# Projection stage of a graph transformer: where ScalarE copies the next turn's normalised features, and where it loads the table of the square root

## What is computed

```
xn  = _layernorm(x, ln1_g[l], ln1_b[l])
deg = (deg - deg.mean()) / (jnp.std(deg, ddof=1) + 1e-06)
pos = xn @ Wpos[l] + bpos[l] + deg[:, None] * Wdeg[l][0] + bdeg[l]
xp  = xn + pos
q   = (xp @ Wq[l] + bq[l]).reshape(n, H, HD)          # k and v alike, by Wk and Wv
att = clip(einsum('ehd,ehd->eh', q[dst], k[src]) / scale, -50, 50)
ex  = exp(att - m[dst])                                # summed and weighted by target node
...
x   = x + (aggr @ Wo[l] + bo[l])
h   = gelu(_layernorm(x, ln2_g[l], ln2_b[l]) @ W1[l] + b1[l])
x   = x + (h @ W2[l] + b2[l])
```

## Time and profile before

| what | before |
|---|---|
| median of 3 runs | 6860.24 us (6857.8 to 6868.34) |
| profiled execution, its own time | 6853.69 us |
| its span in the trace | 6851.9 us |
| busy share PE / DVE / ACT / POOL | 78% / 64% / 43% / 45% |
| projection stage of layer 0 in the span | about 2400 to 2575 us |
| projection stage of layer 1 in the span | about 3885 to 4043 us |

### The profile page before, as it was taken

The page is one execution under the profiler, slowest core; times in us unless marked ns, Lnnn a source line. Parts: engine busy times, 40 slices in busy tenths (PEclk is TensorE's granted clock), DMA queues, the critical chain, the costliest instruction groups (busy, mean ns, idle before and its releaser), DMA issues. The chain is left out here.

```text
span 6851.9 us, 123614 instructions
## 1 busy us (share of the span) xinstructions
PE 5331.7 (78%) x28313; PEld 3586.6 (52%) x28314; DVE 4415.0 (64%) x13076; ACT 2974.1 (43%) x5625; POOL 3066.0 (45%) x3096
## 2 busy tenths in 40 slices
PE   7987995887887656666675767666666999999998
PEld 3443443666666545555554556555555444444433
DVE  8999997888877578888886478888875111000000
ACT  2542551777777325666665335555554000000000
POOL 3763772777777007777773027777760000000000
PEclk9999996999999768999998878899988999999999
DMA  1000002555556216777775036666670677777799
GB/s 24 0 3 1 0 3 62 181 181 180 181 180 167 59 35 211 225 224 224 223 223 116 10 103 205 204 205 206 205 181 30 236 288 288 268 288 286 305 421 388
DMA packets 464533, 1168.30 MB, mean 171 GB/s; under 512 B 112062, under 2 KB 175102, under 8 KB 432156
## 3 DMA queue, kind: packets, MB, share of 16 engines
q1 hardware_dynamic: 337228, 892.75, 35.2%
q0 software_dynamic: 124928, 273.12, 16.2%
q10 hardware_dynamic: 2256, 0.89, 0.1%
HBM read 759.86 MB, written 405.30 MB: 170 GB/s over the span
## 5 line engine op out<-in xcount | busy, mean ns | idle before, releaser
L720 POOL DMA_INDIRECT ACC<-tab_kv,STAGE x1664 | 1632.5, 981 | 1248.5 <-DMA STAGE<-IDX 717.3
L926 PE MATMUL PS<-ITEM 128*128 128x512 f16 x1456 | 590.8, 406 | 585.1 <-ACT PS L1242 583.1
L1242 ACT ACTIVATE PS<-PS,X 128x512 f32<-128x512 f32 x1456 | 964.1, 662 | 167.2 <-PE PS L926 107.3
L720 POOL DMA_INDIRECT SCR<-tab_h,STAGE x832 | 804.9, 967 | 319.1 <-issue 197.8
L1083 PE MATMUL PS<-ACC,Q 128*128 128x512 f32 (+3 forms) x2548 | 843.3, 576 | 49.1 <-DMA ACC<-adj 39.5
L1746 DVE TENSOR_TENSOR ACC<-ACC,PS 128x137 f32 (+1 forms) x2288 | 745.9, 326 | 202.8 <-PE PS L918 68.8
L896 PE MATMUL PS<-Q,SCR 128*128 x4992 | 734.2, 293 | 92.3 <-issue 91.5
L787 PE MATMUL PS<-Q 128*128 128x416 f16 x4160 | 758.1, 341 | 60.5 <-DVE Q L1540 60.5
L896 PEld LDWEIGHTS PS<-Q,SCR 128*128 128x128 f32 x4992 | 682.6, 205 | 208.1 <-issue 184.8
L681 POOL DMA_INDIRECT placed<-ACC,X x576 | 606.6, 1053 | 408.0 <-DVE X L1517 219.5
L914 PE MATMUL PS<-SCR 128*128 128x137 f32 x3328 | 569.2, 321 | 194.7 <-DVE ACC L1746 194.7
(11 more groups left out here) (297 smaller groups left out, 7571.7 us busy)
## 6 DMA issues: line engine op xcount, KB each, us to landing
ACC<-adj SPq DMA_DIRECT2D x252, 1792.0 KB, 6.8
adj<-X SPq DMA_DIRECT2D x936, 256.0 KB
adj<-ITEM SPq DMA_DIRECT2D x520, 256.0 KB
ACC<-tab_kv,STAGE POOLq DMA_INDIRECT x1664
SCR<-tab_h,STAGE POOLq DMA_INDIRECT x832
tab_kv<-SCR SPq DMA_DIRECT2D x14, 896.0 KB, 4.1
ACC<-adj SPq DMA_DIRECT2D x21, 448.0 KB, 3.8
placed<-ACC,X POOLq DMA_INDIRECT x576, 2.3
```

The source lines that it names most:

```text
L720: nc.gpsimd.indirect_dma_start(G[:, q, j, 0:w], None, table, bass.IndirectOffsetOnAxis(STAGE[:, u, q * S4 + j:q * S4 + j + 1], 0))\
L926: nc.tensor.matmul(CLASS_SUM[k % 2], OHS1[:, k % ring, :], OHD[:, k % ring, :], start=False, stop=True, skip_group_check=True).then_inc(ad ...
L1242: nc.scalar.activation(CLASS_SUM[(k + 1) % 2], CLASS_SUM[k % 2], ACT.Copy, scale=KEEP[:, bass.ds(i, 1)])\
```

## The change

One column `ROOT` is allocated. On ScalarE, in both layers, the copy to `T1` of the next turn moves from the head of a loop turn to a place ahead of the exponent (so it is now the copy of turn g + 2 and not of g + 1), the first of these copies moves ahead of the loop, and the one behind the loop goes. At the loop's head a square root of one constant column is taken into `ROOT`, which nothing reads.

```
@@ -156,6 +156,7 @@
+        ROOT = sb("ROOT", [P, 1])[:, :]
@@ -1331,12 +1332,13 @@
                 copied(T1, R[0], s, "xt", "xtc", 0, **norm1)
                 copied(T7, R[0], s, "pt", "ptc", 0)
                 deviation(s, 1)
+                copied(T1, R[0], s, "xt", "xtc", 1, **norm1)
                 with act.Fori(0, NG - 2) as g:
-                    copied(T1, R[0], s, "xt", "xtc", g + 1, **norm1)
+                    nc.scalar.activation(ROOT, EPS[:, 0:1], ACT.Sqrt)
                     copied(T7, R[0], s, "pt", "ptc", g + 1)
                     deviation(s, g + 2)
+                    copied(T1, R[0], s, "xt", "xtc", g + 2, **norm1)
                     self_exp(g)
-                copied(T1, R[0], s, "xt", "xtc", NG - 1, **norm1)
                 copied(T7, R[0], s, "pt", "ptc", NG - 1)
                 self_exp(NG - 2)
                 self_exp(NG - 1)
```

## The result

| | before | changed |
|---|---|---|
| median | 6860.28 us (6857.8 to 6868.34, 6 runs) | 6835.82 us (6830.15 to 6838.42, 6 runs) |
| ratio | | 0.9963, 95% interval 0.9953 to 0.9973 |
| profiled execution, span | 6853.69, 6851.9 | 6835.00, 6833.2 |
| both projection stages, from the traces | 322.94 us | 297.80 us |

The account below looks back on a forecast made before the run. Engines waiting for each other in a ring bound the projection stages, with two VectorE waits in it. Copy 22.2 plus root 7.2 gave 29.4 us less: 6824.3 from the profiled execution, 6830.8 for the median, range 6822 to 6846.

Parts of the forecast that it names:

- What bounds: In the projection stages VectorE waits for the position product (16.1, 16.3 us) and, at the reciprocal, the root (5.5, 5.4 us).
- the ring: In the two projection stages engines wait for each other; none is full, and VectorE waits least.
- The copy, moved: Copy to T1 ahead of the exponent: ten VectorE waits for the position product fall from 24.2 to 2.0, gaining 22.2 us.
- I take 0.2 a turn, 2.0 in all: VectorE's wait left for the position product after the copy moves, over ten turns; bounds 0 and 13 us.
- these two bracket the runs that I looked at: On TensorE, the clock rises between 3.3 and 4.45 us into an unbroken run.
- The bound of 1.3 us a turn: VectorE's wait for the position product if TensorE's clock stays low through that product.
- The root's table: Load hidden in ScalarE's idle time behind the exponent; wait at the reciprocal falls from 1.14 to 0.37 us, gaining 7.2 us.
- The exponent in hand: On ScalarE, moved copy and exponent's table load end 3.0 us before the scores are ready, so they cost nothing.
- The 6.8 us for break-even: Lateness of the transposes ahead of the exponent beyond which the kernel is slower: 3.0 slack plus 3.8 gained a turn.
- The low-clock rival: TensorE's clock stays low through the position product: only 15.9 us less, 6844 us; chance 0.11.
- No gain, and slower: Two rivals: work hidden anyway or wait renamed, 6860 us, chance 0.06; exponent late behind the moved copy, 6872, chance 0.03.

Follow-up runs that it names:

- copy alone: Changed kernel without the early root, only the copy to T1 moved: both stages 301.87 us, median 8851.06 us, ratio 0.9974 to the kernel before.
- root alone: Kernel before with only the early root, put behind the copy to T1: both stages 312.42 us, median 8860.45 us, ratio 0.9987.
- runs with more loads: Changed kernel with two or four more table loads a loop turn, ahead of the exponent: both stages 295.76 and 323.04 us, ratios to before 0.9963 and 0.9994.

## Why the prediction was right or wrong

The forecast was 29.4 us less and 24.5 came, inside the range. By the waits, 3.3 us of the difference lie in the copy's part and 1.1 in a term left out.

- **What bounds.** Right. VectorE's two waits were the ones in the ring; each alone gives its part (21.1 and 10.6 us of stage time), and together 25.1 to 25.4. The parts sum to 31.7, 6.3 us more than both together, because the position waits hang on the clock: 1.4 us in the copy alone and 5.2 in the changed kernel, 20.2 with the root alone and 22.7 to 24.2 before.
- **The copy, moved.** The mechanism was right, and its size was off. The step that failed is "I take 0.2 a turn, 2.0 in all": it was 0.53 a turn, 5.3 us in all. It rested on "these two bracket the runs that I looked at", 3.3 and 4.45 us into the run, and they did not even bracket those of before: one rise was 3.1 us into its run (3950.84 to 3953.9), and in turn 2 of layer 0 (wait 1.90 us) the clock stood high when the run began at 2460.9, fell at 2462.3 and rose again at 2465.7. And both distances were taken from runs that started 5.2 us behind kv, with the product with Wq ahead of them, while the runs of the changed kernel start at kv. In the changed kernel the clock rose 2.9 to 6.2 us into the ten runs of the loop turns. The range held because it went up to the low-clock case; how much was lost inside it is where the rises happened to fall. The bound of 1.3 us a turn held: it was reached in the last loop turn of layer 1 (1.30). The gain was 18.9 and not 22.2 us.
- **A term left out.** The last products also run at the clock that they find. L1903 waits 2.4 us when the run takes 6.55 us and 3.5 us when it takes 7.69, 1.1 us lost in layer 1. The prediction named this wait and gave it no term.
- **The root's table.** Right to 0.1 us: 7.2 us, 0.37 us a time. The load and the new root (0.20 us) lay in ScalarE's idle time.
- **The exponent in hand.** Right: 2.99 us for 3.0. The runs with more loads show that it is 3 us and that beyond it every us is paid. The 6.8 us for break-even added the gain of the one turn shown (3.8); by the prediction's own sum the mean was 29.4 / 10 = 2.9, which gives 5.9, and 6.0 was measured.
- **The low-clock rival** came true in part, as a mixture over turns (it was named so): one turn in ten at its full price, six at 0.4 to 0.9 us, three at nothing.
- **No gain, and slower.** Neither came. The exponent could be made late, by 6.0 us of extra work ahead of it a turn, and then the stages took what they took before; a kernel slower than before by this was not made.

That the rest of the wait is the clock's is shown: with the clock high it is 0 in ten turns of ten. Why the rise came later than forecast is shown in part. The rises of layer 1 lie 20.5 us apart while the runs start 19.4 to 20.3 us apart, so they walk through the run from 4.0 to 6.2 us. That fits a monitor that does not start with the work, as the Trainium skill (TensorE: Matmul & The Clock Gate, The HAM clock gate) has it. What sets where the first rise of a stage falls is not shown.

## What to carry to other kernels

When engines wait for each other in a ring, an engine that takes its instructions in order should do what is ready first: here a copy that had been ready for 7 us stood behind an exponent whose input was not. A load of an activation table costs 1.28 us wherever it stands, so make it stand in idle time; a small operation of the same table, whose result nobody reads, puts it there. And when a bubble on TensorE goes, count the next wait at the low clock too, since how far into a run the clock rises is not the same from turn to turn (2.9 to 6.2 us here).

## What was not expected

- The two projection stages together take the same time to 0.2 us in sessions in which the whole program differs by 2 ms (8.86 and 6.86), in the changed kernel single waits included. The difference lies in the loops of the sort and of the edge passes; I did not look for its cause.
- The compiler puts a table load at the head of a loop even if the first operation in it needs no particular table (behind the loop the kernel before makes the same copy right after the exponent, at 2550.25, with no load): in the copy-alone kernel the loop has three loads in a turn again, the first ahead of the plain copy to `T7`, as before there was one ahead of the copy to `T1`. With the root at the head, the changed kernel has two.
- Moving TensorE's order by one product cost 15 us before the change and gained 3.4 us behind it.
